# A row stride of 1280 instead of 1250 elements for the turned activations of a graph network

## The chip, the cores and the metric

The kernel runs on one NeuronCore of a Trainium2 chip. The metric is the device time of one execution in microseconds (us), taken as the median over runs. Engines are named as in the profile: PE is TensorE's matrix multiply and PEld its weight load, DVE is VectorE, ACT is ScalarE, POOL is GpSimd, SP is SyncE, which issues the transfers.

## The reference, cut to what matters

There are 1250 nodes with 512 features each and 21250 edges. First comes a graph network layer (`L0`): a sum over neighbours and two dense products with a hidden width of 1024. Then come four blocks (`L1`), each with a conditioned layer norm, a four-headed attention over the edges and a two-layer dense network:

```python
for i in range(NUM_BLOCKS):
    y = _cond_layer_norm(x, cond, s1_w[i], s1_b[i], b1_w[i], b1_b[i])
    y = _sparse_attention(y, src, dst, wq[i], bq[i], wk[i], bk[i], wv[i], bv[i], wo[i], bo[i])
    x = x + y
    y = _cond_layer_norm(x, cond, s2_w[i], s2_b[i], b2_w[i], b2_b[i])
    y = jax.nn.relu(y @ m_w1[i] + m_b1[i]) @ m_w2[i] + m_b2[i]
    x = x + y
```

All of it is in float32.

## The kernel before

Nodes lie in ten tiles of 128 rows (NT = 10, the last of 98). NP = 1280 is the ten tiles' full width, N = 1250 the number of nodes. Attention is computed densely over all 1250 nodes, with a mask that holds the logarithm of each edge's count.

The dense products of the blocks are float32 to nearly full precision, made of three passes over fp32r operands. Each operand is split in a rounded part (index 0) and the remainder (index 1). `three_passes` (called at line 1224 for every product of the blocks) multiplies remainder by rounded, rounded by remainder, and rounded by rounded (PARTS), each pass with its own weight load.

The tile that the change touches is `yT`, the normed activations turned so that features lie on the partitions. Its shape is [128, 2, 4, 1250]: two parts, four blocks of 128 features, and the nodes. Each of the eight rows of a partition is thus 1250 elements or 5000 bytes long. It is written, ten node tiles at a time, by a scalar copy at line 698 (part 0) and a vector subtraction at line 1009 (part 1), behind transposes at line 1288. It is read by four products of each block:

- M1, Q and K have weights `w` as the stationary operand and `yT` as the moving one. The nodes go in three groups, GROUPS = (0, 512), (512, 512), (1024, 226). So each of the 12 (feature block, group) pairs takes 4 x 3 = 12 matmuls, 144 per product: 96 with 512 columns and 48 with 226.
- V has 128 nodes of `yT` as the stationary operand and a row of 512 of `w` as the moving one: 10 x 12 = 120 matmuls.

With four blocks this makes 1152 matmuls of 512 columns and 576 of 226 that move `yT`, and 480 that load it as weights.

Three kinds of fp32r products have operands whose rows are a multiple of 1024 bytes long instead. WO and M2 load `kh` [128, 2, 4, 1280] as weights (rows of 5120 bytes) and move `w` (rows of 2048). The scores move `kh` and load `q_parts` (rows of 1024). The neighbour sums of L0 (line 1183) move `counts` (rows of 5120) and load `x_low` or `x_high` (rows of 2048).

All large tiles lie in one slab per partition, in the order of this list:

```python
SLAB = [("x", 20480), ("cond", 5024), ("q", 20480), ("kh", 40960), ("v", 20480), ("yp", 40960), ("q_parts", 4096), ("s_first", 5120),
        ("w", 32768), ("y", 6144), ("film", 4096), ("film_raw", 4096), ("row_bias", 6144)]
```

`yT` is in `yp`, `counts` in `kh`, `x_high` in `w`, `x_low` in `x`. During attention the same `yp` holds `pT` (the first 22528 bytes) and three mask tiles behind it (up to 37888). `yT` before takes 40000 of the 40960 bytes.

PE's instructions run in the order of the job lists (`turned_and_dense`, `qkv_jobs`, `wo_m1_jobs`). PE waits on `dve_out` for the turned tiles before M1 and Q, and in `bank_of` for the PSUM bank to be copied out.

Of the kernel before, what the change touches and what calls it, by code (L numbers as in the profile page):

```python
# [11 lines left out]
F32R = mybir.dt.float32r  # L12
# [4 lines left out]
P = 128  # L17
N = 1250
# [5 lines left out]
KD = D // P  # L24
NT = -(-N // P)
NP = NT * P
# [143 lines left out]
def gnn_kernel(nc, x_in, src, dst, noise, W1, b1, W2, b2, eps0, f_w1, f_b1, f_w2, f_b2, s1_w, s1_b,  # L170
# [51 lines left out]
    with ExitStack() as ctx:  # L222
# [30 lines left out]
        def at(part, plus, name, shape, dt=F32):  # L253
            return nc.alloc_sbuf_tensor_at(name, shape, dt, offset=offset[part] + plus)
# [3 lines left out]
        q = at("q", 0, "q", [P, KD, N])  # L258
        kh = at("kh", 0, "kh", [P, 2, KD, NP], F32R)
        v = at("v", 0, "v", [P, NT, D])  # L260
        yT = at("yp", 0, "yT", [P, 2, KD, N], F32R)
        pT = at("yp", 0, "pT", [P, 2, NT + 1, 2 * P])
        masks = [at("y", 0, "mask_y", [P, NP]), at("w", 0, "mask_w", [P, NP])] + [
            at("yp", 22528 + 5120 * n, f"mask_{n}", [P, NP]) for n in range(3)]
# [1105 lines left out]
```

## Time and profile before

| | us |
|---|---|
| median of 3 runs | 1933.54 |
| lowest, highest | 1930.05, 2387.07 |
| span of the profiled execution | 1927.7 |
| PE busy in it | 1867.7 (97%) |
| PEld busy | 1559.8 (81%) |
| DVE busy | 1115.2 (58%) |
| ACT busy | 713.7 (37%) |
| POOL busy | 339.7 (18%) |

The highest run is a disturbed one; the other two agree within 3.5 us. The profiled span lies 5.8 us below the median and 2.4 below the lowest. PE's busy time is no measure of how well it is used, since matmuls overlap and their ends are modelled. How fast PE goes is read from the starts: a row that merges n matmuls gives the start of the first and the time to the end of the last. So its length less one matmul's duration, by n - 1, is the gap from one start to the next.

### The profile page before, as it was taken

What the parts mean: (1) busy time and instruction counts of PE and PEld (TensorE: products, weight loads), DVE (VectorE), ACT (ScalarE), POOL (GpSimd) and SP (SyncE); (2) the same over time, 40 slices, a digit from 0 to 9 for tenths busy, and PEclk for the clock granted to TensorE, in tenths of its full rate; (3) what the DMA queues carried; (4) which work ended last, traced back from release to release, by engine and by line L of the source; (5) the groups of instructions that cost most, each with busy time, mean ns of one, the idle gap of its engine ahead of it and who ended that gap; (6) DMA issues with size and microseconds to landing.
All of it is one profiled execution on the core that took longest, in us unless ns stands there. A gap on an engine that the chain in (4) does not pass through costs nothing.

```text
span 1927.7 us, 31229 instructions
## 1 busy us (share of the span) xinstructions
PE 1867.7 (97%) x11066; PEld 1559.8 (81%) x11067; DVE 1115.2 (58%) x2389; ACT 713.7 (37%) x924; POOL 339.7 (18%) x395
## 2 busy tenths in 40 slices
PE   4999999999999999989999999999999999999998
PEld 4888654687888888878888888788888887888887
DVE  6998735634555567345554773355548734455476
ACT  2112230113565441125554412256553312556532
POOL 3000541400000344000001540000016300000063
PEclk8999999999999999999999999999999999999999
DMA  3001301121100111210101011201010112000011
GB/s 117 0 0 58 131 0 55 49 76 48 36 28 1 38 38 35 76 43 22 48 1 38 23 50 37 83 14 39 17 38 23 43 43 82 14 28 28 23 65 65
DMA packets 38730, 79.63 MB, mean 41 GB/s; under 512 B 10856, under 2 KB 10856, under 8 KB 38592
## 3 DMA queue, kind: packets, MB, share of 16 engines
q1 hardware_dynamic: 38592, 77.82, 11.7%
q8 instruction: 83, 1.36, 0.3%
q14 instruction: 55, 0.45, 0.1%
HBM read 66.14 MB, written 11.67 MB: 40 GB/s over the span
## 4 chain that ended last, share of the span: by engine, by line
PE 65%; issue 32%; DVE 1%; POOL 1%; ACT 1%; POOLq 0%; ACTq 0%; DVEq 0%; PEldq 0%
PE ps L1224 38%; PE ps L1158 6%; PE ps L1249 5%; PE ps L1282 4%; PE ps L1214 4%; PE ps L1332 2%; PE ps L1275 2%; PE ps L1183 2%; PE ps L1288 2%; POOL film L518 0%; ACT counts L631 0%; POOL kh L571 0%; DVE s L940 0%; PE ps L1333 0%; PE ps L1145 0%
## 5 line engine op out<-in xcount | busy, mean ns | idle before, releaser
L1249 PE MATMUL ps<-pT,v 128*128 128x256 f32 (+1 forms) x1600 | 364.2, 375 | 3.0 <-ACT pT L736 3.0
L675 ACT ACTIVATE s<-s,small 128x1280 f32<-128x1280 f32 (+1 forms) x156 | 212.8, 1364 | 341.7 <-DVE small L943 341.7
L1224 PE MATMUL ps<-yT,w 128*128 128x512 f32 (+1 forms) x1728 | 335.5, 355 | 0.0
L1224 PE MATMUL ps<-kh,q_parts 128*128 128x512 f32 (+3 forms) x1440 | 318.3, 366 | 5.7 <-DVE v L1025 3.4
L1224 PEld LDWEIGHTS ps<-yT,w 128*128 128x128 f32 x1728 | 281.5, 190 | 49.3
L1249 PEld LDWEIGHTS ps<-pT,v 128*128 128x128 f32 x1600 | 292.6, 190 | 31.9 <-ACT pT L736 3.9
L1224 PEld LDWEIGHTS ps<-kh,q_parts 128*128 128x128 f32 (+1 forms) x1440 | 246.1, 187 | 52.1 <-issue 4.8
L1224 PE MATMUL ps<-w,kh 128*128 128x512 f32 (+1 forms) x960 | 235.2, 396 | 1.9 <-POOL kh L571 1.9
L736 ACT COPY pT<-ps 128x1408 f32<-128x1408 f32 (+1 forms) x160 | 208.8, 1305 | 9.1 <-PE ps L1333 5.5
L940 DVE CUSTOM_DVE_ANT_0 s<-ps,mask 128x1280 f32<-128x1280 f32 x96 | 143.2, 1492 | 113.6 <-PE ps L1224 113.6
L1224 PEld LDWEIGHTS ps<-w,kh 128*128 128x128 f32 (+1 forms) x960 | 174.4, 186 | 40.6 <-POOL kh L571 2.5
L1332 PE MATMUL ps<-ident,s 128*128 128x128 f32 (+1 forms) x1560 | 191.9, 270 | 1.9 <-ACT pT L736 1.9
L1332 PEld LDWEIGHTS ps<-ident,s 128*128 128x128 f32 (+1 forms) x1560 | 176.7, 141 | 16.4 <-issue 2.2
L571 POOL TENSOR_TENSOR kh<-q,kh 128x512 fp32r<-128x512 f32 (+1 forms) x40 | 46.5, 1168 | 786.6 <-ACT kh L669 786.5
L698 ACT CAST yT<-ps 128x512 fp32r<-128x512 f32 x80 | 45.5, 579 | 318.6 <-PE ps L1288 318.6
L1158 PE MATMUL ps<-hot 125*128 125x128 bf16 x1960 | 124.3, 223 | 18.8 <-DVE hot L823 8.7
L1158 PEld LDWEIGHTS ps<-hot 125*128 125x128 bf16 x1960 | 113.6, 100 | 29.5 <-DVE hot L823 16.5
L1078 DVE TENSOR_SCALAR small<-small 128x1 f32<-128x1 f32 (+1 forms) x160 | 24.6, 154 | 183.1 <-ACT s L675 175.6
L821 DVE TENSOR_SCALAR hot<-iota_n,edge 125x1280 bf16<-125x1280 f16 x196 | 117.3, 598 | 14.4 <-PE ps L1158 11.7
L1224 PE MATMUL ps<-w,yT 128*128 128x512 f32 (+1 forms) x480 | 112.3, 393 | 0.0
L1224 PEld LDWEIGHTS ps<-w,yT 128*128 128x128 f32 (+1 forms) x480 | 88.5, 186 | 21.2
L560 POOL TENSOR_TENSOR x<-x,row_bias_t 128x512 f32<-128x512 f32 x80 | 102.8, 1294 | 0.3 <-DMA x_first<-x 0.3
(164 smaller groups left out, 1958.4 us busy)
## 6 DMA issues: line engine op xcount, KB each, us to landing
mask<-mask_dram SPq DMA_DIRECT2D x24, 640.0 KB, 4.4
w_raw<-in_L_gnn_m_w_dram SPq DMA_DIRECT2D x8, 1024.0 KB, 5.5
mask_y<-mask_dram SPq DMA_DIRECT2D x12, 640.0 KB, 4.1
mask_dram<-mask_out SPq DMA_DIRECT2D x10, 640.0 KB, 2.9
w_l<-in_L_gnn_W_dram SPq DMA_DIRECT2D x2, 2048.0 KB, 9.8
w_raw<-in_L_gnn_wq_dram SPq DMA_DIRECT2D x4, 1024.0 KB, 5.5
w_raw<-in_L_gnn_wk_dram SPq DMA_DIRECT2D x4, 1024.0 KB, 5.4
w_raw<-in_L_gnn_wv_dram SPq DMA_DIRECT2D x4, 1024.0 KB, 5.4
```

What stands on the lines that cost most here:

```text
L560: nc.gpsimd.tensor_tensor(x[0:R, t, :], x[0:R, t, :], row_bias[0:R, row, :], ALU.add).then_inc(biased, 1)
L571: nc.gpsimd.tensor_tensor(kh[:, 1, :, tile], q[:, :, tile], kh[:, 0, :, tile].bitcast(F32), ALU.subtract).then_inc(o_ready, 1)
L675: nc.scalar.activation(s_of(u), s_of(u), ACT.Exp, bias=small[0:R, u % 2, 1:2], accum_out=small[0:R, u % 2, 2:3]).then_inc(exp_done, 1)
L736: nc.scalar.copy(pT[:, gh % 2, :, k * P:k * P + R], turn[:, :, 0:R]).then_inc(pT_out, 1)
L821: nc.vector.tensor_scalar(hot[0:ET, m, 0:NP], iota_n[0:ET], edge[:, 0, bass.ds(t + m, 1)], None, ALU.is_equal)
L940: nc.vector.tensor_tensor_reduce(s_of(u), ps_flat[0:R, 0:NP], masks[MASK_PLACE[t]][0:R, :], 1.0, LOWEST, ALU.add, ALU.max, small[0:R, u % ...
L1158: mine = mm(ps_flat[:, c0:c0 + P], hot[0:ET, m, i * P:(i + 1) * P], hot[0:ET, m, NP:NP + P], start=first and m == 0 and i % 4 == 0, stop=T ...
L1214: mine = mm(bank[:, 0:cn], w1_l0[:, k, a * P:(a + 1) * P], q[:, k, c0:c0 + cn], start=(k == 0), stop=(k == KD - 1))
L1224: mine = mm(to, left(a), right(b), start=first and n == 0, stop=final and n == 2)
L1249: mine = mm(ps[:, 6 + gh % 2, 0:wd], v[:, t, h * P:(h + 1) * P], pT[:, gh % 2, t, 0:wd], start=(t == 0), stop=(t == NT - 1))
L1282: mine = mm(bank[0:R, :], hidden[:, k, a * P:a * P + R], w2_l0[:, k, :], start=(k == 0), stop=(k == H1 // P - 1))
L1332: nc.tensor.transpose(turn[:, t * P:t * P + R], s_of(u)[:, t * P:(t + 1) * P], ident[0:R, 0:R])
```

## The change

The last dimension of `yT` goes from N (1250) to NP (1280) elements. Each row is then 5120 bytes long and the tile fills the 40960 bytes of `yp` exactly. No instruction is added, removed or moved, and no access reads or writes the 30 elements of padding.

```diff
@@ -258,7 +258,7 @@
         q = at("q", 0, "q", [P, KD, N])
         kh = at("kh", 0, "kh", [P, 2, KD, NP], F32R)
         v = at("v", 0, "v", [P, NT, D])
-        yT = at("yp", 0, "yT", [P, 2, KD, N], F32R)
+        yT = at("yp", 0, "yT", [P, 2, KD, NP], F32R)
         pT = at("yp", 0, "pT", [P, 2, NT + 1, 2 * P])
```

## Rows read from the trace of the kernel before

**Rows 1.** Groups of PE by shape: busy us, mean ns of one, idle before:

```profile
line engine op names shapes xcount | busy us, mean ns | idle before us <-releasers
L1224 PE MATMUL ps<-yT,w 128*128 128x512 f32 x1152 | 271.8, 395 | 0.0
...
L1224 PE MATMUL ps<-w,kh 128*128 128x512 f32 x864 | 211.4, 395 | 1.9 <-POOL kh L571 1.9
...
L1224 PE MATMUL ps<-w,yT 128*128 128x512 f32 x432 | 101.2, 393 | 0.0
...
L1224 PE MATMUL ps<-yT,w 128*128 128x226 f32 x576 | 66.2, 274 | 0.0
...
L1183 PE MATMUL ps<-counts,x_low 128*128 128x512 f32 x72 | 18.3, 398 | 2.2 <-ACT counts L631 2.2
L1183 PE MATMUL ps<-counts,x_high 128*128 128x512 f32 x72 | 17.8, 391 | 0.0
```

**Rows 2.** Waits of PE in the whole span: total us, times, longest:

```profile
PE ps L1158 <- DVE hot L823: 8.7, 1, 8.7
...
PE ps L1332 <- DVE rep L1085: 4.9, 2, 2.5
PE ps L1224 <- DVE v L1025: 3.4, 4, 0.9
```

**Rows 3.** Timeline of PE: steady stretches of K (first row) and V:

```profile
790.28 9.90 PE L1224 MATMUL ps<-yT,w 128*128 128x512 f32 x42
```

```profile
811.63 20.74 PE L1224 MATMUL ps<-w,yT 128*128 128x512 f32 x89
```

**Rows 4.** Timeline of PE: one WO tile whole, and its last nine matmuls alone:

```profile
663.86 2.90 PE L1224 MATMUL ps<-w,kh 128*128 128x512 f32 x12
```

```profile
664.33 2.21 PE L1224 MATMUL ps<-w,kh 128*128 128x512 f32 x9
```

**Rows 5.** Timeline of PE: neighbour sums of 512 columns, `x_high`, then `x_low`:

```profile
194.44 1.98 PE L1183 MATMUL ps<-counts,x_high 128*128 128x512 f32 x8
```

```profile
196.73 2.04 PE L1183 MATMUL ps<-counts,x_low 128*128 128x512 f32 x8
```

**Rows 6.** Timeline of PE: matmuls of 226 columns, M1's group first:

```profile
777.96 4.74 PE L1224 MATMUL ps<-yT,w 128*128 128x226 f32 x41
```

```profile
205.53 1.05 PE L1183 MATMUL ps<-counts,x_low 128*128 128x226 f32 x8
```

```profile
206.64 1.17 PE L1183 MATMUL ps<-counts,x_high 128*128 128x226 f32 x9
```

**Rows 7.** Groups of DVE and ACT that write or read `yT`, and like ones:

```profile
L1037 DVE TENSOR_TENSOR x<-ps,x 128x512 f32<-128x512 f32 x72 | 49.5, 687 | 49.3 <-PE ps L1224 44.6 <-POOL x L608 4.7
L1009 DVE TENSOR_TENSOR yT<-ps,yT 128x512 fp32r<-128x512 f32 x72 | 48.2, 670 | 1.3 <-ACT yT L698 1.3
```

```profile
L698 ACT CAST yT<-ps 128x512 fp32r<-128x512 f32 x72 | 42.4, 589 | 318.6 <-PE ps L1288 318.6
...
L669 ACT CAST kh<-q 128x512 fp32r<-128x512 f32 x36 | 20.8, 622 | 0.0
```

**Rows 8.** Stretches at the openings of attention, blocks 2, 3, 1, 4; PEclk after the counts:

```profile
846.00:850.00 4.00, 4.00 (x18) 3.25 (x17) 1.90 (x6) 2.64 (x4) 0.00 (x0) 0.58 0.47 186
1239.00:1243.00 4.00, 4.00 (x18) 3.48 (x16) 1.72 (x6) 2.82 (x4) 0.00 (x0) 0.57 0.23 94
453.00:457.00 4.00, 3.45 (x22) 2.90 (x21) 1.65 (x3) 1.31 (x2) 1.67 (x1) 1.00 1.00 405
1629.00:1633.00 4.00, 2.97 (x19) 2.31 (x17) 2.37 (x7) 2.29 (x3) 0.73 (x1) 1.00 0.85 346
```

**Rows 9.** Timeline of PE between V and attention in block 2:

```profile
834.62 5.73 PE L1224 MATMUL ps<-w,yT 128*128 128x512 f32 x24
841.22 2.00 PE L1224 MATMUL ps<-kh,q_parts 128*128 128x512 f32 x9 [0.87 <-DVE v L1025]
845.72 1.48 PE L1332 MATMUL ps<-ident,s_first 128*128 128x128 f32 x10 [2.50 <-DVE rep L1085]
```

## The prediction

> **What bounds the kernel now.** I read the engines' busy shares first: PE is busy for 97% of the span, and no other engine for more than 58%. Then the waits of PE: over the whole span the longest single wait is 8.7 us, in the edge counting of L0, and at line 1224, where all products of the blocks stand, the largest sum is 3.4 us [rows 2]. The groups by shape agree: the matmuls that move or load `yT` have no idle time before them at all [rows 1]. So PE's own pace sets the end in every stage that the change touches, and a nanosecond saved per matmul is a nanosecond off the span, as long as the other engines keep up.
>
> The durations in the groups do not show that pace. They are 395 and 393 ns for 512 columns whatever the operands [rows 1], since matmuls overlap and their ends are modelled. I therefore worked it out from the timeline, from stretches that hold one kind of matmul only: the merged row's length, less one duration, by the count less one. All stretches below are at full granted clock (2.4 GHz), at which 512 columns take 512 / 2.4 = 213.3 ns.
>
> - K, which moves `yT`: (9.90 - 0.395) / 41 = 231.8 ns [rows 1, 3].
> - V, which loads `yT` as weights and moves `w`: (20.74 - 0.393) / 88 = 231.2 ns [rows 1, 3].
> - WO, which loads `kh` and moves `w`, once settled: (2.21 - 0.395) / 8 = 226.9 ns [rows 1, 4].
> - The neighbour sums with `x_high`: (1.98 - 0.391) / 7 = 227.0 ns; with `x_low`: (2.04 - 0.398) / 7 = 234.6 ns [rows 1, 5].
>
> The same kind of instruction, with the same columns, thus goes at three paces: 227, 231 to 232, and 234.6 ns. What differs between them is where the operands lie. I take remainders by 1024 bytes from the slab's list. From `kh` to `w` it is 111616 bytes, 109 x 1024, so `counts` and `x_high`, and `kh` and `w`, start every row at the same remainder or 512 from it. Those are the fast ones. `x_low` lies 45984 bytes before `counts`, which leaves 928; it is the slow one. The rows of `yT` are 5000 bytes long, 4 x 1024 + 904, so its eight rows fall at eight different remainders, and its pace lies between.
>
> **The change, part by part.** Only the row length changes. `yp` is 61440 = 60 x 1024 bytes behind `kh`, and 5120 is 5 x 1024, so every row of `yT` gets the remainder that `kh`, `counts`, `w` and `q_parts` have. That is the case of the 227 ns rows, on both sides: moving, as `counts` against `x_high`, and stationary, as `kh` in WO.
>
> *Moving `yT`, 512 columns* (M1, Q, K): 1152 matmuls x (231.8 - 226.9) = 5.6 us [rows 1, 3, 4].
>
> *Loading `yT`* (V): 480 x (231.2 - 226.9) = 2.1 us [rows 3, 4].
>
> *Settling.* The fast pace is not there at once behind another kind of matmul. The whole WO tile starts at 663.86 and its last nine at or after 664.33, so its first two gaps took 0.47 us, 235 ns each [rows 4]. I charge three gaps at 8 ns more, 0.025 us, for each of the 20 runs that follow another kind (five to a block: two openings of M1, two of Q, one of V's end). That is 0.5 us back.
>
> *Moving `yT`, 226 columns*: here the pace is (4.74 - 0.274) / 40 = 111.7 ns, and the neighbour sums give (1.05 - 0.274) / 7 = 110.9 with `x_low` and (1.17 - 0.274) / 8 = 112.0 with `x_high` [rows 1, 6]. The placement that costs 7.6 ns at 512 columns costs nothing here, so I take nothing. Bounds: the worst is 576 x (112.0 - 111.7) = +0.2 us; the best is the settled surplus of the wide ones, 226.9 - 213.3 = 13.6 ns over 226 / 2.4 = 94.2, which is 107.8 ns and 576 x 3.9 = 2.2 us less.
>
> *The writes of `yT`* by ACT and DVE go to other addresses. The ACT copy takes 589 ns and the DVE subtraction 670; a like copy into `kh`, whose rows are already 5120 bytes, takes 622, and a like DVE sum 687 [rows 7]. So no gain is in sight, and if they rose to these it would be 33 and 17 ns for each of 80. ACT sat idle for 318.6 us before these copies, so it has room, and PE shows no wait on them [rows 2, 7]. If that cover were gone, the loss would be 80 x 0.05 = 4 us. I take zero. Transfers, queues and semaphores stay as they are.
>
> *What comes late next.* V ends sooner, and behind it PE waits for DVE's copy of V's last tile (0.87 us) and for the first softmax (2.50) [rows 9]. Both waits run from PE's own last matmuls onward, through DVE and ACT, so they move with PE and don't eat the gain.
>
> *The clock.* At the openings of attention the granted clock reads 0.58 and 0.57 over 4 us in blocks 2 and 3, and 1.00 in blocks 1 and 4 [rows 8], although PE pauses in all four. Each dip is about 3.4 us at the lower level (1.2 instead of 2.4 GHz), so 4 x 0.42 = 1.7 us lost. What PE did before it fell was to pause for 2.50 us [rows 9]. Whether one falls may depend on where in time the pause lies, and the change moves every pause by some us. I leave two dips in; none would give 3.4 us back, four would cost as much.
>
> Sum: 5.6 + 2.1 - 0.5 = 7.2 us. Against the profiled execution, 1927.7 - 7.2 = 1920.5 us of span. The median is 5.8 us above that span, which I leave: 1933.5 - 7.2 = 1926.3 us, or 0.4% less.
>
> **Two rules beside the rows.** The Trainium skill, "TensorE: Matmul & The Clock Gate", section "Back-to-back issue gap", gives a gap of N / 2.4 + 2.5 ns, 216 ns for 512 columns, with no term for where the operands lie; under "Step-by-step: what each phase is for" it says that loading weights takes nothing from the running matmul, as PE has two separate read ports. By these the change brings nothing, and the time would be 1933.5. The traces do not agree: the rows stand at 226.9 to 234.6. "SBUF — State Buffer", section "Door 1: The DMA port swizzle", has lines of 16 bytes; 5000 is no multiple of 16, so every other row of `yT` starts in the middle of a line and 512 columns touch one line more. It gives no price for that. `x_low` does not fit it, being slow with rows of 2048 bytes that all start alike.
>
> **The rivals.**
>
> *B, no effect.* Two causes would do it. The pace could hang on the kind of run: the 227 ns stretches are ten or twelve matmuls long, the `yT` ones 48 to 240, and nothing shows that the fast pace lasts. Or it could hang on something in `w` that moves from product to product. Against it: eight gaps in a row at 226.9 with no drift, and `x_low` and `x_high`, ten each, in turn on the same moving rows. Time: 1933.5.
>
> *C, slower.* The equal remainders could be a bad pairing for these operands: weight loads of 512 bytes and a stream of 2048 that meet at the same remainder, as the unlucky pair `counts` and `x_low` does at its own distance. The pace would be that of `x_low`: 1632 x (234.6 - 231.6) = +4.9 us, 1938.4 [rows 3, 5]. It decides against me from 231.6 ns on. To make the kernel over 2% slower (38.7 us) it would have to reach 231.6 + 23.7 = 255 ns, which no full-clock stretch that I read comes near. Against it: `kh` with `w` and `counts` with `x_high` have this very pairing and are the fastest.
>
> *D, more than forecast.* The 226 columns gain too (2.2 us) and both dips go (3.4 us): 1920.7. A gain over 2% would need 38.7 us of 1632 matmuls, 23.7 ns each, which is below the 213.3 ns of the columns themselves. It is excluded by this mechanism.
>
> *E, the change does nothing.* All readers take the tile's own row length, so it can't be without effect on the addresses; this falls under B.
>
> **How the numbers follow.** Forecast (some 5 to 9 us less) 0.66; B 0.17; C 0.09; D 0.06; something unseen that is over 2% either way 0.02. About 2% is what a measurement of this kernel can tell from no change. Forecast, B, C and D all lie within it, so: faster 0.01, same 0.97, slower 0.02 with what is left over. The range goes from D's lower half, with the 3.5 us by which the two good runs differ, to B and half of C: 1918 to 1936.
>
> **What would show each step.** The timeline of K and V in the new trace should give gaps of 227 to 228 ns; M1's 226-column stretch should stay at 111 to 112; WO, the scores and attention should not move at all; the copies at lines 698 and 1009 may change by some tens of ns with no PE wait behind them. The span should be near 1920.5. I am wrong if K stays at 231 to 232 (B), if it goes above (C), or if the gaps fall and the span doesn't, which would point to a wait of PE at line 1224 that is absent now, or to more clock dips.

## The result, and the profile after

The changed kernel takes 1924.25 us (median of 6 runs, 1923.54 to 1926.06), beside 1932.15 for the kernel before (6 runs). The ratio is 0.9963, with a 95% interval of 0.9952 to 0.9975. By the ratio that is 7.1 us less, and by its interval 4.8 to 9.3, where 7.2 was forecast; the times alone could not tell the forecast from one 2 us off. One run of the kernel before, at 2387.07 us, was disturbed and is left out of the ratio. The profiled span is 1922.0 us, 5.7 less than before.

The same stretches as in [rows 3] (timeline of PE: start, length to the end of the last, the matmuls and their count), K first, then V:

```profile
790.24 9.00 PE L1224 MATMUL ps<-yT,w 128*128 128x512 f32 x39
814.68 14.67 PE L1224 MATMUL ps<-w,yT 128*128 128x512 f32 x64
```

The durations come from the groups by shape:

```profile
L1224 PE MATMUL ps<-yT,w 128*128 128x512 f32 x1152 | 266.5, 391 | 0.0
...
L1224 PE MATMUL ps<-w,yT 128*128 128x512 f32 x432 | 99.5, 390 | 0.0
```

Take one duration off each length and divide by the count less one. K goes at (9.00 - 0.391) / 38 = 226.6 ns where it went at 231.8, and V at (14.67 - 0.390) / 63 = 226.7 ns where it went at 231.2. That is the settled pace of WO in [rows 4].

What should have stayed did. The rows are first M1's matmuls of 226 columns, then two whole tiles of WO:

```profile
778.04 3.51 PE L1224 MATMUL ps<-yT,w 128*128 128x226 f32 x30
...
661.72 2.90 PE L1224 MATMUL ps<-w,kh 128*128 128x512 f32 x12
664.94 2.90 PE L1224 MATMUL ps<-w,kh 128*128 128x512 f32 x12
```

The narrow ones take (3.51 - 0.274) / 29 = 111.6 ns, as in [rows 6], and WO's tiles 2.90 us, as in [rows 4]. The waits behind V and at the openings of attention are the same to a tenth of a microsecond ([rows 2]):

```profile
PE ps L1332 <- DVE rep L1085: 4.8, 2, 2.4
PE ps L1224 <- DVE v L1025: 3.4, 4, 0.9
```

A few shorter ones inside attention differ: at line 1332 those for ACT's `pT` sum to 2.9 us where they were 1.9, and at line 1224 those for DVE's `small` to 1.8 where they were 2.3.

From the first matmul of each run on `yT` to the first of what follows it, 447.96 us before have become 440.80 (the starts of all such runs in both traces, summed). That is 7.16 us. The span shows only 5.7 of them, for a reason outside the change. The next rows are stretches of the kernel before (their columns: the stretch, its length, busy time and count of each engine, the granted clock, DMA share and GB/s):

```profile
62.00:68.00 6.00, 4.24 (x75) 4.01 (x73) 4.64 (x16) 1.23 (x1) 0.00 (x0) 1.00 0.00 0
...
168.00:176.00 8.00, 7.63 (x33) 6.23 (x34) 4.86 (x6) 3.31 (x3) 0.00 (x0) 1.00 0.20 82
```

and of the kernel after, with the opening of attention in block 3 as well:

```profile
62.00:68.00 6.00, 4.25 (x47) 4.08 (x45) 4.47 (x13) 1.23 (x1) 0.00 (x0) 0.72 0.00 0
...
168.00:176.00 8.00, 6.65 (x22) 5.36 (x23) 3.21 (x4) 3.08 (x3) 0.00 (x0) 0.79 0.20 82
...
850.00:1234.00 384.00, 380.89 (x2091) 329.04 (x2088) 212.21 (x446) 160.87 (x211) 62.70 (x74) 1.00 0.11 34
1234.00:1240.00 6.00, 3.42 (x20) 2.73 (x20) 3.02 (x10) 2.31 (x3) 0.55 (x1) 1.00 0.65 229
```

In L0, before any code that the change touches, two short dips of the granted clock came in. They stand at waits of PE of 1.8 and 2.2 us for ACT's `counts`, which the kernel before has just as long, without a dip. The dip at 1239 us of [rows 8] is gone, and the one of block 2 stays. So this profiled run carries one dip more. The prediction priced a dip at 1.7 us. Both traces hold the same 11066 matmuls, so that each start can be compared with its own: the two new dips put PE back by 1.5 us each, the missing one gave 1.2, and 0.5 had been gained before 55 us. That makes 7.16 - 3.0 + 1.2 + 0.5 = 5.9, close to the 5.7 of the spans.

### The profile page after: what moved, and what is told of

Read it like the earlier page. It is cut to its first block, busy times and chain, and to the rows that moved or that the text cites. A ratio compares the mean times of both kernels' runs of the same rounds, so it can differ in the third digit from the quotient of the medians.

```text
span 1922.0 us, 31229 instructions
## 1 busy us (share of the span) xinstructions
PE 1861.7 (97%) x11066; PEld 1559.5 (81%) x11067; DVE 1116.4 (58%) x2389; ACT 713.5 (37%) x924; POOL 339.6 (18%) x395
## 4 chain that ended last, share of the span: by engine, by line
PE 65%; issue 32%; DVE 1%; POOL 1%; ACT 1%; POOLq 0%; DVEq 0%; ACTq 0%; PEldq 0%
PE ps L1224 38%; PE ps L1158 6%; PE ps L1249 5%; PE ps L1282 4%; PE ps L1214 4%; PE ps L1183 2%; PE ps L1332 2%; PE ps L1275 2%; PE ps L1288 2%; POOL film L518 0%; ACT counts L631 0%; POOL kh L571 0%; DVE s L940 0%; PE ps L1333 0%; PE ps L1145 0%
## 5 line engine op out<-in xcount | busy, mean ns | idle before, releaser
L1224 PE MATMUL ps<-yT,w 128*128 128x512 f32 (+1 forms) x1728 | 330.1, 352 | 0.0
L1158 PEld LDWEIGHTS ps<-hot 125*128 125x128 bf16 x1960 | 115.0, 100 | 29.4 <-DVE hot L823 16.6
```

Source lines behind the costliest of these rows:

```text
L1158: mine = mm(ps_flat[:, c0:c0 + P], hot[0:ET, m, i * P:(i + 1) * P], hot[0:ET, m, NP:NP + P], start=first and m == 0 and i % 4 == 0, stop=T ...
L1224: mine = mm(to, left(a), right(b), start=first and n == 0, stop=final and n == 2)
```

## The experiments

Theory D: the distance between the starts of a matmul's two operands decides its pace. Its rivals were L, that each row's own start decides (whether it lies on 16 bytes), and K, that the kind of run decides and addresses do nothing.

**All rows on 16 bytes, but at different remainders.**

```diff
-        yT = at("yp", 0, "yT", [P, 2, KD, NP], F32R)
+        yT = at("yp", 0, "yT", [P, 2, KD, 1252], F32R)
```

> yT's rows 1252 elements, 5008 bytes: every row starts on a multiple of 16 bytes, but at eight different remainders by 1024 (steps of 912). Theory L: as fast as the changed kernel, 227 ns in K and V, span near 1920 to 1922. Theory D: about as slow as 5000 bytes, 231 to 232 in K and V, span near 1927 to 1929.

Measured, in one run: span 1930.4 us, time 1932.17, beside 1932.65 for the kernel before. The timeline, K and then V:

```profile
790.18 9.03 PE L1224 MATMUL ps<-yT,w 128*128 128x512 f32 x38
814.67 14.50 PE L1224 MATMUL ps<-w,yT 128*128 128x512 f32 x62
```

K goes at (9.03 - 0.395) / 37 = 233.4 ns and V at (14.50 - 0.393) / 61 = 231.3. Starting each row on a multiple of 16 bytes brings nothing, so L by itself falls. A coarser step, 32 bytes for instance, is not excluded by this run, since 5008 is no multiple of 32; the next one settles that.

**The distance put back by a gap, with rows of 5120 bytes.**

```diff
-        SLAB = [..., ("yp", 40960), ("q_parts", 4096), ...
+        SLAB = [..., ("yp", 40960), ("gap", 96), ("q_parts", 4096), ...
```

> The changed kernel with 96 unused bytes between yT's region and the weights', so that every three-pass product of the blocks has its two operands 96 bytes apart from a multiple of 1024 (q_parts moves along, so the scores too); rows stay 5120 bytes long. Theory D: the pace of x_low, 234.6 instead of 227, at 1632 matmuls that touch yT, 960 of WO and M2 and 960 of the scores with 512 columns: about 3552 x 7.6 = 27 us more than the changed kernel, 1951, slower than the kernel before (1.01). Theory L: nothing changes, since 96 is a multiple of 16: 1924. Theory K: nothing changes: 1924.

Measured: 1940.62 us (1940.46 to 1941.14), ratio to the kernel before 1.0043 (1.0026 to 1.0060). It is slower than both kernels although `yT` has its padded rows. K and V, and then WO's tiles:

```profile
790.26 9.06 PE L1224 MATMUL ps<-yT,w 128*128 128x512 f32 x38
814.82 14.40 PE L1224 MATMUL ps<-w,yT 128*128 128x512 f32 x61
...
662.51 2.96 PE L1224 MATMUL ps<-w,kh 128*128 128x512 f32 x12
665.78 2.96 PE L1224 MATMUL ps<-w,kh 128*128 128x512 f32 x12
```

K is at (9.06 - 0.397) / 37 = 234.1 ns, V at 233.5. The neighbour sums with `x_high`, now also 96 bytes from `counts`, take 2.51 us for ten, as `x_low` does. L and K have no place for this: every row here starts on a multiple of 32 bytes, and no product changed in kind. The size was missed: 16.4 us over the changed kernel and not 27. From start to start, against the second trace of the changed kernel (below), whose dips lie at the same openings, the runs on `yT` took 10.6 us more, where 1632 x 7.6 = 12.4 was forecast. WO and M2 took 4.3 more for 7.3, and the scores 3.3 for 7.3. What the forecast left out is that the first gaps of a run cost much the same at both distances. A score has only six matmuls of 512 columns in a row, and only its last two gaps rose, from 227 to 231 and 232 (medians).

**The same gap, 256 bytes wide.**

```diff
-        SLAB = [("x", 20480), ("cond", 5024), ("q", 20480), ...
+        SLAB = [("x", 20480), ("cond", 5024), ("q", 20224), ...
-                ("yp", 40960), ("q_parts", 4096), ...
+                ("yp", 40960), ("gap", 256), ("q_parts", 4096), ...
```

> The changed kernel with 256 unused bytes between yT's region and the weights', taken from the unused end of q's place. Every three-pass product of the blocks now has its operands 256 bytes from a multiple of 1024 apart, where weights_96_on had 96. If whole multiples of 256 are free, as in the tables of paces: the same gaps as the changed kernel (227.3 ns moving yT, 227.5 loading it) and the same time, 1924 to 1926. If only a multiple of 1024 is free, or if any gap in the slab costs what weights_96_on cost: 1938 to 1941.

> The changed kernel itself, beside weights_256_on on the same chip: 1924 to 1926, and gaps of 227.3 ns where yT is moved. It gives the yardstick for the comparison, and a second trace in which the places of the clock's dips can be compared with the first.

Measured: 1923.48 us (1921.42 to 1928.05) for the gap and 1923.80 (1920.42 to 1925.61) for the changed kernel on the same chip, with 1930.63 for the kernel before; ratios 0.9959 (0.9945 to 0.9973) and 0.9962 (0.9947 to 0.9976). K and V of the kernel with the gap:

```profile
790.28 9.00 PE L1224 MATMUL ps<-yT,w 128*128 128x512 f32 x39
814.72 14.45 PE L1224 MATMUL ps<-w,yT 128*128 128x512 f32 x63
```

That is 226.6 and 226.8 ns. The gap itself costs nothing; 96 bytes did, 256 don't. In this trace and in the second one of the changed kernel the runs on `yT` sum to 440.81 us, as against 440.80 in the first. A gap of 192 bytes, which the tables below have between free and slow, has no room in the slab as it stands and was not measured in the whole kernel.

**Everything moved on by 96 bytes together.**

```diff
-        SLAB = [("x", 20480), ("cond", 5024), ...
+        SLAB = [("x", 20480), ("cond", 5120), ...
```

> The changed kernel with cond's place in the slab 5120 instead of 5024 bytes long: all that lies behind it moves on by 96 bytes together, so that yT, w, kh and q_parts keep their distances and the whole of counts, x_low and x_high now has one remainder. Theory D: the blocks keep 227 ns, and the sums with x_low go from 234.6 to 227, 80 matmuls x 7.6 = 0.6 us less: 1923.6. Theory L and one in which the absolute start decides (the fast rows begin at 32 over a multiple of 64, and no longer would): the blocks' products go to 231 or more, 1930 and above.

Measured: 1925.40 us (1924.32 to 1926.27), ratio to the kernel before 0.9965 (0.9951 to 0.9979), no different from the changed kernel's. The blocks kept their pace (K again 39 matmuls in 9.00 us). The neighbour sums, `x_low` and then `x_high`:

```profile
193.71 2.46 PE L1183 MATMUL ps<-counts,x_low 128*128 128x512 f32 x10
196.00 2.46 PE L1183 MATMUL ps<-counts,x_high 128*128 128x512 f32 x10
```

In [rows 5] `x_low` was the slow one. Moved to the remainder of `counts`, it takes what `x_high` takes: over all its matmuls of 512 columns the mean gap fell from 234.5 to 229.5 ns. That saves 80 x 5 = 0.4 us, too little for the time to show.

**A table of paces.** This kernel leaves out all of the computation. PE runs alone, one kind of matmul 40 to 96 times in a row, each with its weight load. A line of it, 96 bytes apart, is

```python
for i in range(80): last = nc.tensor.matmul(ps[:, 4, 0:512], st[:, 0, 0, 24:152], mv[:, 0:512], start=(i == 0), stop=(i == 79))
```

> This kernel leaves all of the computation out. It runs PE alone: 40 to 96 matmuls in a row of one kind, with a weight load each, at chosen distances between the starts of the stationary and the moving operand. Theory D (the distance between the two starts decides): fp32r at 512 columns settles at 226.7 to 227 ns with distance 0 and with both operands moved on together by 8, 32 or 96 bytes; at 96 bytes apart it stands near 234.6; rows of 5000 bytes, moved or loaded in the order of the real products, give 231 to 232, rows of 5120 give 227. At 226 columns there is nothing between them (111 to 112). Theory L (each row's own start decides, by whether it lies on a multiple of 16 bytes): 16, 32, 96 and 128 bytes apart are as fast as 0, while 8 bytes apart, and both moved on by 8 bytes, are slow. Theory K (the kind of run decides, not the addresses): every case of 512 columns has one pace.

> Again PE alone, all of the computation left out; each kind of matmul on its own line, 80 or 96 in a row. What the first table leaves open: which distances are free, what both operands moved on together does, from which width on the distance counts, and what sets the 226-column pace. Theory D256 (free where the distance is a multiple of 256 bytes and both starts lie on 16 bytes): 227 ns at 0, 256, 512, 768 and 1280 bytes apart, 229 to 235 at 240, 264, 272, 288, 320; both moved on by 16, 64 or 128 bytes 227, by 4, 8, 12 or 24 about 231. Theory D1024 (only whole 1024): 256, 512 and 768 slow; the first table speaks against it. Widths: the first table has 384 and below immune and 512 not, so the edge lies between 400 and 508. If the narrow ones are bound by the weight load, 228 and 232 columns still take 111.7 ns, and from about 236 on the gap follows columns / 2.4 + 13.3 (240: 113.3, 248: 116.7). If not, 228 to 248 rise one by one from 111.7. With 98 or 64 weight columns at 96 bytes apart: slow as with 128 if the two reads meet anywhere, less so if the length of the load counts.

Rows of the second table (timeline of PE; each line of the code is one case, and the next case's start less this one's, by the count, is the pace):

```profile
45.41 18.30 PE L63 MATMUL ps<-mv,st 128*128 128x512 f32 x80
63.54 18.62 PE L64 MATMUL ps<-mv,st 128*128 128x512 f32 x80
...
100.40 18.90 PE L66 MATMUL ps<-mv,st 128*128 128x512 f32 x80
119.14 18.84 PE L67 MATMUL ps<-mv,st 128*128 128x512 f32 x80
...
193.08 18.32 PE L71 MATMUL ps<-mv,st 128*128 128x512 f32 x80
211.24 18.62 PE L72 MATMUL ps<-mv,st 128*128 128x512 f32 x80
...
395.94 18.83 PE L82 MATMUL ps<-mv,st 128*128 128x512 f32 x80
414.60 18.84 PE L83 MATMUL ps<-mv,st 128*128 128x512 f32 x80
433.28 18.30 PE L84 MATMUL ps<-mv,st 128*128 128x512 f32 x80
451.41 18.34 PE L85 MATMUL ps<-mv,st 128*128 128x512 f32 x80
...
778.82 9.10 PE L105 MATMUL ps<-mv,st 128*128 128x232 f32 x80
787.76 9.10 PE L106 MATMUL ps<-mv,st 128*128 128x236 f32 x80
...
897.51 22.40 PE L114 MATMUL ps<-long,wt 128*128 128x512 f32 x96
919.75 21.95 PE L115 MATMUL ps<-even,wt 128*128 128x512 f32 x96
941.53 22.35 PE L116 MATMUL ps<-wt,long 128*128 128x512 f32 x96
963.72 21.93 PE L117 MATMUL ps<-wt,even 128*128 128x512 f32 x96
```

Line 63 is 0 bytes apart: (63.54 - 45.41) / 80 = 226.6 ns. Line 66 is 96 apart: (119.14 - 100.40) / 80 = 234.3. Line 71 is 256 apart: (211.24 - 193.08) / 80 = 227.0, first gaps included. Lines 114 to 117 are the rows of 5000 and of 5120 bytes, moved and then loaded, in the order of the real products: (919.75 - 897.51) / 96 = 231.7, (941.53 - 919.75) / 96 = 226.9, (963.72 - 941.53) / 96 = 231.1, and 227 for the last. They are the paces of M1, Q, K and V before and after, with no other engine at work. Settled gaps of all cases, from both tables: the mean of the starts' differences after the first eight of each case. "Apart" is how far the stationary operand starts behind the moving one, counted from a multiple of 1024 bytes:

| fp32r, 512 columns | ns |
|---|---|
| 0, 256, 512, 768, 1280 bytes apart | 226.7 |
| 192, 240 apart | 228.9, 228.3 |
| 24, 8, 264 apart | 230.0, 230.7, 230.7 |
| 4, 128, 384 apart | 232.3, 232.7, 232.3 |
| 16, 32, 48, 64, 160, 224, 272, 288, 320 apart | 233.3 |
| 96 apart | 234.2 to 234.4 |
| the moving operand on instead, by 8, 32, 96, 128 | 233.4, 233.3, 233.3, 232.6 |
| both moved on by 32, 64, 96, 128 | 226.7 to 227.0 |
| both moved on by 12, 8, 16, 24, 4 | 228.9, 231.1, 233.3, 233.3, 237.8 |

Theory D in the form "whole multiples of 1024" was too narrow: multiples of 256 bytes are free, and the paces repeat after 256. 264, 272, 288, 320 and 384 apart take what 8, 16, 32, 64 and 128 take, within 0.4 ns. So the side counts too: the moving operand on by 32 and 96 is the case of 224 and 160 apart, 233.3 ns each. The kernel with the gap of 96 bytes shows both sides: in K the weights start 96 behind the moving rows (234.1 ns), in V 96 before them (233.5).

The theory was also incomplete. With both operands moved on together by 16 bytes (line 82: (414.60 - 395.94) / 80 = 233.3 ns) the distance is zero and the pace is still slow, while by 64 (line 84) it is fast, (451.41 - 433.28) / 80 = 226.6. So a start has to lie well too: every start that is fast is a multiple of 32 bytes, and here L was half right, with a coarser step than its own.

| other kinds, 0 and 96 bytes apart | ns |
|---|---|
| fp32r, 384 columns | 173.3, 173.3 |
| fp32r, 320 | 146.7, 146.7 |
| fp32r, 256 | 120.0, 117.4 |
| fp32r, 226 | 111.6, 111.7 |
| fp32r, 128 | 111.7, 111.6 |
| fp32, 512, each of its two instructions | 429.2, 429.2 |
| bf16, 512 | 215.8, 215.8 |

Two records are missing from that trace, near its end, and the bf16 value at 96 bytes leaves out the double gap where one should stand. Between 400 and 508 columns there is no order: 400 takes 180.0 and 182.2, 448 takes 206.7 both, 504 takes 226.7 both, 508 takes 227.6 and 233.3. With 98 weight columns both distances give 231 to 232 ns; with 64 the one 96 apart is the faster (226.6, and 230.1 with no distance). So the free distances are a finding on 128 weight columns and 512 moved ones, and no rule for other shapes.

**What bounds the narrow group.** 128, 226, 228, 232 and 236 columns all take 111.7 ns (line 105: (787.76 - 778.82) / 80 = 111.8). Then it rises: 240, 244, 248 and 256 columns take 112.0, 113.2, 115.0 and 120.0, somewhat below columns / 2.4 + 13.3 at first (113.3 and 116.7 were expected at 240 and 248). Below some 240 columns the pace doesn't depend on the columns. That fits a bound by the weight load that each matmul brings, but no run has narrow fp32r matmuls with a shorter load or none, so the reason is argued and only the floor is shown. 226 columns thus pay for about 240. From this a better split follows:

```diff
-GROUPS = [(0, 512), (512, 512), (1024, N - 1024)]
-TILES_OF = [range(0, 4), range(4, 8), range(8, NT)]
+GROUPS = [(0, 512), (512, 384), (896, N - 896)]
+TILES_OF = [range(0, 4), range(4, 7), range(7, NT)]
```

(the two waits that turn a tile's number into its group follow this split).

> The changed kernel with the nodes in groups of 512, 384 and 354 columns instead of 512, 512 and 226. If a gap is columns / 2.4 + 13.3 ns down to some 236 columns and 111.7 ns below (the weight load), three matmuls take 226.7 + 173.3 + 160.8 = 560.8 instead of 226.7 + 226.7 + 111.7 = 565.1 ns, 4.3 ns less for each of the 576 such triples of M1, Q and K, 2.5 us, and 0.3 us in the neighbour sums: about 1921.5, ratio 0.9985 to the changed kernel. If 226 columns are bound by their columns, the sum is the same and so is the time: 1924.3.

> groups_384_354 and all_96_on together: every fp32r product at one remainder. If both hold, 2.8 + 0.5 us less than the changed kernel, near 1921, and faster than both kernels. The clock's dips of 1.7 us each can hide that.

The second and third group of M1 in block 1 (timeline), 96 matmuls; the changed kernel first:

```profile
703.32 16.53 PE L1224 MATMUL ps<-yT,w 128*128 128x512 f32 x96
```

and with the new groups:

```profile
701.99 16.25 PE L1224 MATMUL ps<-yT,w 128*128 128x384 f32 x96
```

That is 0.28 us less for 48 pairs, from the first start to the last end. Summed over all runs that move `yT`, the trace shows 327.5 us before and 324.6 after the edit, 2.9 less, for 2.5 forecast. The time doesn't resolve it. Both were measured beside 1933.04 for the kernel before: the groups alone 1925.25 us (1920.34 to 1931.25), ratio 0.9964 (0.9950 to 0.9977), no better than the changed kernel's 0.9963, and with everything at one remainder 1922.25, ratio 0.9943 (0.9930 to 0.9957). So 1921.5 was forecast for the first and not seen in the time. The second has the lowest ratio of all that were tried, but its interval overlaps that of the changed kernel (0.9952 to 0.9975). Its runs go from 1917.76 to 1927.10, and the granted clock from 0.995 down to 0.992 with them. The shorter runs on `yT` are shown by the starts; a faster kernel is likely, and not shown.

## Why the prediction was right

- **The bound.** PE alone set the end of every stage touched, and a nanosecond saved per matmul was one off the chain: no wait of PE came in at the runs on `yT`, and those behind them stayed what they were.
- **Moving `yT`, 5.6 us forecast.** The mean gap of these 512-column matmuls (over all gaps of the trace under 250 ns, which leaves out each run's first) fell from 232.0 to 227.3 ns: 1152 x 4.7 = 5.4 us.
- **Loading `yT`, 2.1 us.** From 231.4 to 227.5: 480 x 3.9 = 1.9 us.
- **Settling, 0.5 us back.** It is inside the two means above. They lie 0.7 and 0.8 ns over the settled 226.6 and 226.7 after, and 0.2 over 231.8 and 231.2 before, so settling took 1152 x 0.5 + 480 x 0.6 = 0.9 us, not 0.5. In return the settled paces fell by 5.2 and 4.5 ns and not by 4.9 and 4.3, which is 0.4 us more. That the two misses cancel, so that the starts give 7.16 beside a forecast of 7.2, is in part luck; each term by itself was right in kind and within half a microsecond. The nine matmuls of WO in [rows 4] are also not the tile's last nine but its third to eleventh: 664.33 is the start of the third. The reading of the first two gaps, 235 ns each, stands by this, and 226.9 contains one gap that had not settled.
- **226 columns, nothing.** Right: 111.6 and 111.6. The tables show what lies behind it: so narrow, their columns do not set their pace.
- **The writes.** The copy at line 698 went from 589 to 587 ns and the subtraction at 1009 from 670 to 668. Neither bound was needed.
- **The waits behind V** moved with PE, as said: 0.9 us at DVE's copy of V's last tile in both traces.
- **The clock.** "I leave two dips in" was wrong for the profiled run, which has three, and two of them lie in L0, where I had not looked for any. The second trace of the changed kernel has two, in blocks 2 and 3 as before. The price of 1.7 us was a little high: by the starts they cost 1.2 to 1.5.
- **Rival B** (the fast pace does not last, or hangs on the kind of run) is refuted by the gap of 96 bytes, which makes the same runs slow again, and by 96 matmuls in a row at 226.9. **Rival C** named a true mechanism at the wrong place: equal remainders are the good pairing, and the pace of `x_low` is what 96 bytes cost.
- **The durations.** "395 and 393 ns for 512 columns whatever the operands" was too quick a reading. The same rows have 391 for `x_high` and 398 for `x_low`, and with one kind of run alone the duration moves with the gap: in the second table it is 389 ns at a gap of 226.7, 396 at 234.2 and 399 at 237.8. It is not the pace, and a group's mean mixes in the openings of its runs (WO has 395 at a settled gap of 227). Nothing in the sum hangs on it.
- **What the prediction had too narrow** was the rule behind its numbers. It took remainders by 1024 since all the fast pairs of that trace shared one; 256 is enough. That didn't matter for a tile whose rows can only be 1250 to 1280 elements long, in which 1280 is the only multiple of 256 bytes.
- **The Trainium skill's two rules.** The section "Back-to-back issue gap" in the Trainium skill's "TensorE: Matmul & The Clock Gate" gives 216 ns for 512 columns. The tables agree for bf16 (215.8) and not for fp32r (226.7 at best, 237.8 at worst). The section "Step-by-step: what each phase is for" of the same page of the Trainium skill has weight loads take nothing from the running matmul. The fp32r rows do not fit that, since the pace follows the distance between the stationary and the moving operand. They do not disprove it either, as no run here leaves the weight loads out.

That the addresses decide is shown, by the gap of 96 bytes and by PE alone. The cause beneath was not settled. A guess is that the two reads of PE meet in the memory, which would fit the period of 256 bytes. It explains neither the starts on 32 bytes, nor why 384 and 504 columns are immune, nor why 64 weight columns turn the order round. The runs show when it is slow, not why.

## What to carry to other kernels

Where TensorE is the bound and fp32r matmuls of 512 columns with full weight loads run back to back, start both operands on multiples of 32 bytes, let their rows be multiples of 256 bytes long and let their starts differ by such a multiple: here rows of 5000 bytes instead of 5120 cost 2% of each such matmul. Measure it from one start to the next, in a stretch of one kind. The duration column only hints at it: the group of 1152 went from 395 to 391 ns. Count the columns of the last group too: an fp32r group of 128 to 236 columns, with full weight loads, took the 112 ns of one with 240.

## What the runs showed that was not expected

- An fp32r matmul of 512 columns has a surplus over its columns' 213.3 ns that ranges from 13.3 ns to 24.5 with the addresses alone, while bf16 and fp32 take the same at 0 and 96 bytes apart (215.8 ns, and 429.2 for each of fp32's two instructions).
- Shifting both operands by the same 4 bytes costs 11 ns a matmul (237.8), more than any distance between them that was tried.
- The granted clock fell for about 3.4 us at waits of PE of about 2 us, in places that changed from run to run of the same code: at 62 to 68 us it read 0.72 in one run of the changed kernel, and in another 1.00, with the same wait of 1.8 us in both:

```profile
62.00:68.00 6.00, 4.24 (x76) 4.01 (x74) 4.64 (x16) 1.23 (x1) 0.00 (x0) 1.00 0.00 0
```

In the first of the two traces such a dip cost 1.2 to 1.5 us, about a fifth of what this change brings, so a gain of this size is better read from the starts of the matmuls than from one span.
